# Final layer norm of output rows 0 to 13 on ScalarE with a scale and a bias per token, instead of on GpSimd

## What is computed

```python
def _layernorm(x, axis=-1, eps=1e-05):
    m = jnp.mean(x, axis=axis, keepdims=True)
    v = jnp.var(x, axis=axis, keepdims=True)
    return (x - m) / jnp.sqrt(v + eps)

x = _layernorm(x + _L0_attn_ref(x, ...))
x = _layernorm(x + _L0_xattn_ref(x, ctx_512, ctx_512))
x = _layernorm(x + _L0_ffn_ref(x, ...))
return x
```

## Time and profile before

| | us |
|---|---|
| three runs | 767.22, 767.64, 771.85 |
| median | 767.64 |
| the profiled execution, device time | 770.78 |
| its span, first to last instruction | 769.0 |
| PE busy (share of the span) | 738.5 (96%) |
| DVE busy | 577.0 (75%) |
| ACT busy | 450.5 (59%) |
| POOL busy | 385.0 (50%) |

### The profile page before, as it was taken

How to read it: one execution, slowest core, us unless ns; L and a number is a source line. 1 busy time by engine, 2 the same in 40 slices (tenths; PEclk the granted TensorE clock), 3 DMA queues, 4 the chain that set the end, 5 groups by cost and what they waited for, 6 DMA issues and landing times. The chain is left out here.

```text
span 769.0 us, 17459 instructions
## 1 busy us (share of the span) xinstructions
PE 738.5 (96%) x5978; PEld 412.5 (54%) x5978; DVE 577.0 (75%) x1134; ACT 450.5 (59%) x883; POOL 385.0 (50%) x439
## 2 busy tenths in 40 slices
PE   8899999999999999999999999999589999999897
PEld 3456555565555655556565555666324444356554
DVE  5676867778676686867668688796678899877687
ACT  7744437644454764445575454555347788858476
POOL 2876626544443573533449755564212321459654
PEclk9999999999999999999999999999879999989999
DMA  6675232426324132621423224320040000000001
GB/s 204 198 210 178 56 59 51 107 47 162 80 55 93 44 82 55 177 78 45 95 55 84 69 60 113 71 62 1 14 187 23 16 22 23 23 0 3 28 29 56
DMA packets 34299, 57.92 MB, mean 75 GB/s; under 512 B 7056, under 2 KB 11920, under 8 KB 33680
## 3 DMA queue, kind: packets, MB, share of 16 engines
q1 hardware_dynamic: 33680, 57.08, 28.2%
q10 hardware_dynamic: 576, 0.31, 0.1%
HBM read 54.10 MB, written 2.36 MB: 73 GB/s over the span
## 5 line engine op out<-in xcount | busy, mean ns | idle before, releaser
L285 POOL TENSOR_TENSOR cum_rows<-cum_rows,cum_t 128x512 f32<-128x512 f32 x128 | 136.6, 1077 | 194.2 <-DMA cum_rows<-cum_scratch 194.2
L788 PE MATMUL pring<-xt_hi,w_hi 128*128 (+1 forms) x576 | 171.6, 380 | 0.0
L788 PE MATMUL pring<-xt_lo,w_hi 128*128 (+1 forms) x576 | 171.3, 379 | 0.0
L788 PE MATMUL pring<-xt_hi,w_lo 128*128 (+1 forms) x576 | 171.3, 379 | 0.0
L650 DVE TENSOR_TENSOR bt<-pring,bt 128x512 f16<-128x512 f32 x128 | 88.1, 688 | 72.2 <-ACT bt L442 72.2
L442 ACT CAST bt<-pring 128x512 f16<-128x512 f32 x128 | 74.6, 583 | 111.3 <-PE pring L788 111.1
L654 DVE TENSOR_TENSOR ct<-pring,ct 128x512 f16<-128x512 f32 x128 | 88.2, 689 | 53.7 <-ACT ct L446 53.5
L830 PEld LDWEIGHTS pscore<-ct,bt 128*128 128x128 f16 x1536 | 96.0, 98 | 33.9 <-issue 6.1
L830 PE MATMUL pscore<-ct,bt 128*128 128x128 f16 x1536 | 106.6, 219 | 3.2 <-issue 1.6
L446 ACT CAST ct<-pring 128x512 f16<-128x512 f32 x128 | 74.8, 585 | 52.5 <-PE pring L788 52.5
L1330 DVE TENSOR_REDUCE mx<-bank_at 128x4 f32<-128x512 f32 x128 | 83.6, 689 | 15.8 <-PE bank_at L1539 14.7
(11 more groups left out here) (154 smaller groups left out, 994.5 us busy)
## 6 DMA issues: line engine op xcount, KB each, us to landing
cum_rows<-cum_scratch SPq DMA_DIRECT2D x32, 1024.0 KB, 7.9
w_raw<-in_w_in SPq DMA_DIRECT2D x35, 256.0 KB, 7.0
q_rows<-in_xt SPq DMA_DIRECT2D x4, 512.0 KB, 10.7
acc<-in_x SPq DMA_DIRECT2D x1, 2048.0 KB, 7.5
vals<-in_vals SPq DMA_DIRECT2D x16, 128.0 KB, 2.1
out<-acc SPq DMA_DIRECT2D x7, 256.0 KB, 2.1
w_raw_e<-in_w_up SPq DMA_DIRECT2D x1, 1024.0 KB, 5.0
w_raw_e<-in_w_gate SPq DMA_DIRECT2D x1, 1024.0 KB, 7.0
```

The lines of the kernel that those rows point to most:

```text
L285: nc.gpsimd.tensor_tensor(rows[:, par, :, q], rows[:, par, :, q], own, ALU.subtract).then_inc(sem("since"), 1)
L788: mm = nc.tensor.matmul(bank[name][:], w[:, c, k, cols], x[:, k, bass.ds(n % TB, 1), :].rearrange("p o n -> p (o n)"), start=(i == 0), sto ...
```

## The change

POOL's `finish(i)` no longer normalises the rows of a pair. It still takes the power, and then makes one more small instruction, `shift3 = -mean * rstd`. DVE prepares `-mean` with one more small instruction in `final_aggr`. ACT normalises each row with one ACTIVATE of the function Identity, `acc = rstd * acc + shift`, with scale and bias as per-token pointers. It does so at fixed places of its list: row 2k after unit 8 + 4k, row 2k + 1 after unit 9 + 4k (behind the evacuations of that unit), rows 12 and 13 after the last `evac_hidden`. Each waits for `shift` of its pair. Rows 14 and 15 stay on DVE and count on a semaphore of their own, `last_rows`.

```diff
+        shift3 = sb("shift3", [P, BATCH], F32)
@@ sync
             for g in finals:
-                sp.wait_ge(sem("final"), g[-1] + 1)
+                if len(g) > 1:
+                    sp.wait_ge(sem("final"), g[-1] + 1)
+                else:
+                    sp.wait_ge(sem("last_rows"), g[0] - BATCH + 3)
@@ gpsimd, finish(i)
                 if len(finals[i]) > 1:
                     pool.wait_ge(sem("ln3_rstd"), i + 1)
-                    for b in finals[i]:
-                        nc.gpsimd.tensor_scalar(acc[:, b], acc[:, b], mean_var3[:, b, 0:1], rstd3[:, b:b + 1], ALU.subtract, ALU.mult).then_inc(sem("final"), 1)
+                    nc.gpsimd.tensor_tensor(shift3[:, finals[i][0]:finals[i][-1] + 1], shift3[:, finals[i][0]:finals[i][-1] + 1], r, ALU.mult).then_inc(sem("shift"), 1)
@@ scalar
+            def final_row(b):
+                act.wait_ge(sem("shift"), b // 2 + 1)
+                nc.scalar.activation(acc[:, b], acc[:, b], ACT.Identity, bias=shift3[:, b:b + 1], scale=rstd3[:, b:b + 1]).then_inc(sem("final"), 1)
@@ scalar, at the end of the loop over users
+                b, odd = divmod(u - 8, 4)
+                if b >= 0 and odd < 2:
+                    final_row(2 * b + odd)
             evac_hidden(UNITS - 1)
+            for b in range(BATCH - 4, BATCH - 2):
+                final_row(b)
@@ vector, final_aggr(i)
+                nc.vector.tensor_scalar(shift3[:, r], mean_var3[:, r, 0], -1.0, None, ALU.mult)
                 nc.vector.tensor_scalar(rstd3[:, r], mean_var3[:, r, 1], EPS, None, ALU.add).then_inc(sem("ln3_var"), 1)
@@ vector, final_rows(i)
-                    ... .then_inc(sem("final"), 1)
+                    ... .then_inc(sem("last_rows"), 1)
```

More of the change, by code:

```diff
@@ L1478, in final_rows @@
                 for b in finals[i]:
-                    nc.vector.tensor_scalar(acc[:, b], acc[:, b], mean_var3[:, b, 0:1], rstd3[:, b:b + 1], ALU.subtract, ALU.mult).then_inc(sem("final"), 1)
+                    nc.vector.tensor_scalar(acc[:, b], acc[:, b], mean_var3[:, b, 0:1], rstd3[:, b:b + 1], ALU.subtract, ALU.mult).then_inc(sem("last_rows"), 1)
             bias_scores(0)
```

## The result

| | before | after |
|---|---|---|
| runs, us | 767.22, 767.64, 771.85, 772.83 | 776.11, 777.92, 781.97, 782.42 |
| median, us | 769.75 | 779.94 |
| ratio, 95% interval | | 1.0119 [1.0075, 1.0162] |
| profiled span, us | 769.0 | 774.3 |

(Before has one run more than was known for the prediction.) The change makes the kernel slower, by 9.2 us by the ratio. The forecast was 775.5 from 767.64, +7.85 or 1.0102; 767.64 x 1.0119 is 776.8, which lies inside the range of 771.8 to 779.5 and just above the narrower 774.6 to 776.6 of the forecast itself.

What follows compares the result with a forecast made beforehand. No engine alone was taken to bound the experts: PE, DVE and ACT hand units to each other. 5.83 + 0.45 + 0.27 + 1.3 = 7.85 us, from 767.64 to 775.5, range 771.8 to 779.5.

Steps and rivals of the forecast that it cites:

- Stall: At unit 8, ACT's row 0 waits for POOL's shift of pair 0, making Silu of unit 9 5.83 us late.
- A row: Each normalising ACTIVATE with two pointers occupies ACT for 0.49 us, 0.61 from start to end; bounds 0.39 to 0.61.
- Creep: Rows on ACT delay three dense cycles by 0.45 us together, and DVE's negation adds 0.27: 0.72 us.
- the negation's 0.27: DVE's added instruction costs 0.09 us per pair, counted three times where DVE has no gap; 0.8 if never covered.
- The account that was to confirm the 0.15: In a dense cycle of four units, two rows take 0.98 us of ACT against 0.91 spare.
- The covers: Row 1 hides behind PE's router work, rows 2 to 5 in ACT's waits or DVE's routing: 0; uncovered, 0.49 each.
- The clock: After PE's six idle microseconds behind unit 8, its clock falls to 1.2 GHz, costing 1.3 us; bounds -1.3 to 3.4.
- POOL's relief: POOL loses 17 us of work that no one needs: gain 0, at most 0.35 us at the end.
- POOL is in time: Rival: shift of pair 0 is there by 706.9, so no stall; 768.4 us, no change; chance 0.04.
- another table: Rival: Identity needs another function table, two loads for each of 14 rows; about 804 us; chance 0.03.
- A long low stretch: Rival: low clock reaches over the router's matmuls too, or a row costs its upper bound; 777 to 779.5; chance 0.22.
- No net clock loss: Rival: the stall comes, but PE keeps its clock or the fall moves there from behind the router; 774.2; chance 0.26.

Runs made afterwards that it cites:

- two kernels without the stall: The changed kernel with rows 0 and 1 normalised on ACT behind unit 10, ratio 1.0001; the changed kernel with pair 0 left on POOL, ratio 1.0020 to before.
- the filled kernel: The changed kernel with 50 more matmuls of 128x256, whose result nobody reads, on PE in front of turn_x(7); ratio 1.0055 to before, 776.65 us.
- finish(0) earlier: The changed kernel with finish(0) moved ahead of split_x(2) and cast_x(2) in POOL's list; ratio 1.0012 to before.
- router split: The kernel before with the second router block's 32 small matmuls cut in two halves, expert_up(11) between them; ratio 0.9993 to before.

## Why the prediction held, and where it was off

The mechanism was right: the stall, its place and its size, and the small creep. That the total came so near was in part luck with the clock. The first series gives +9.2 us by the ratio, the second, of the same kernel, +11.8 (1.0153, or 779.4 from 767.64), which is still inside the range, at its very edge.

The steps, against what was measured from unit 8 on in the two executions of the changed kernel:

- **Stall, 5.83 predicted, 5.71 and 5.69 measured.** POOL's order, the place of the wait, and that ACT idles until POOL's multiplication is through all came as read from the earlier trace rows. The one unknown, the small multiplication, was put at 0.3 and took 0.20.
- **A row, 0.49 predicted, 0.50 measured.** From start to end 0.61 was predicted; row 0, alone, took 0.60, and the rows in the dense units are printed with 0.63 to 0.67, which gives the mean of 0.633. So the second pointer costs about as much as the first, and the lower bound of 0.39 is ruled out. The Trainium skill ("ScalarE: Activation LUTs", section What ACT_TABLE_LOAD costs) says that each pointer operand adds about 93 ns. The trace agrees: 0.60 less the 0.417 of a source without pointers is 0.09 for each.
- **Creep, 0.72 predicted, 0.68 and 0.69 measured** in the two kernels without the stall. The cycle of 7.14 us is the predicted 6.99 + 0.15, and the negation's 0.27 was 0.22 in the kernel that had it alone. The account that was to confirm the 0.15 did so only roughly: it gives 0.98 - 0.91 = 0.07, and it took a unit of ACT for 1.52 us where ACT can do 1.47. The covers held: units 12 to 16, with rows 2 and 3, take 10.10 us in both kernels, units 16 to 20, with rows 4 and 5, 10.37 instead of 10.33. Behind row 1 no wait of PE is printed at `turn_hidden(10)`.
- **The clock, 1.3 predicted, 1.9 and 3.4 measured.** This is the term that was mis-sized, and with it the total: 8.3 and 9.8 us in the profiles instead of 7.85. I priced one fall by its cost to `expert_up(11)` through `down(9)` alone, 1.26 us, though the low level in the earlier trace rows goes on into S2, and a whole fall costs 1.7, as the filled kernel shows. And I let the fall behind the stall be as short as that one, while it lasted longer in all three executions that had it (the granted clock is 0.50 from 709 to 715 after, and from 715 to 718 behind the router's block of before). In the second execution the fall behind the router was a long one as well. The stall isn't shown to be the reason for that, since two kernels without a fall at the stall (finish(0) earlier, router split) had a long one too. Both were in my bounds, not in the value.
- **POOL's relief, 0 predicted, none seen.** POOL idles before its last instruction, 1.32 us instead of 0.35, and DVE's row 15 still waits 0.45 us for the power of its own row.
- **The rivals.** "POOL is in time" and "another table" fell with the first profile. "A long low stretch" (777 to 779.5) is what the second execution shows; the first series, at 776.8, lies between it and the forecast. "No net clock loss" came only where PE was given work in its gap.

What stays open: why the clock falls behind the router's block for a short time in one execution and a long one in another, why it doesn't fall there at all in the filled kernel, whose block is the same, and why it fell behind a gap of 2.27 us in router split only. The long falls had begun well inside the block: its 32 matmuls take 4.59 us in the kernel with finish(0) earlier against 3.64 in the earlier trace rows. The time of the changed kernel varies with it.

## What to carry to other kernels

An engine with a low share of busy time can still be late: what counts for a new wait is where the producer stands in its own list at that moment, and POOL, idle for half of the span, had 9 us of work ahead of pair 0. Price a moved instruction in two parts, its work and its new wait; here 7 us of work cost 0.7, and one wait of 5.4 us cost 5.7 before the clock is counted, while the same two rows placed two units later, in a gap that ACT had anyway, cost nothing to speak of. When the wait makes TensorE stand still, add what the clock takes afterwards, at its measured length and to the end of the low stretch.

## What the runs showed of the hardware

TensorE's clock is a term of its own size. Gaps of 5.1 to 5.9 us ended at 1.2 GHz in all three executions that had them, and one of 1.67 us left the level at 2.4 GHz. A gap of 2.27 us left it there in the kernel before and was followed by a fall in router split, so the length of a gap alone doesn't tell it. And 5.6 us of useless matmuls in such a gap made the kernel 5.8 us faster in the median.

It also goes with part of the spread of the runs. In kernels that are the same up to there, Silu of unit 8 started anywhere from 702.1 to 707.4 us. In the profile of after, the first tanh to Silu of unit 4 took 13.97 us with the level at 1.00 throughout; in that of before it took 15.43, with a fall behind the first router block. A comparison of two profiled spans (5.3 us here) would have missed a third of the loss; the distance between two instructions around the change doesn't.
